# Four chained transformer-like layers on one core: layer 0's two softmax units interleaved, layer 1's keys moved, loads reordered, spare products on TensorE at both ends, a new order of stages

## What is computed

```python
# layer 0: 16 query heads, one key/value head, windowed softmax, gate, RMS norm, centring over tokens
probs = softmax(where(window, q @ k.T * scale, NEG)); attn = (probs @ v) @ Wo + bo
gate = silu(concat(attn, x) @ Wg + bg); out = attn * gate + x * (1 - gate)
x1 = rms(out) * rms_w; x1 = x1 - mean_over_tokens(x1)
# layer 1: each token looks at the three context rows around its index
w = square(relu(q1 . k1[idx-1 .. idx+1] / 4)); x2 = x1 + (w / sum(w) @ v1) @ Wo1
# layer 2: self attention (16 heads, relative bias), then cross attention to the context
xa = x2 + attention(x2, x2); x4 = xa + attention(xa, ctx)
# layer 3: a Mamba2 block in its quadratic form, then cross attention with 8 heads
x5 = x4 + mamba(x4); out = x5 + cross_attention(x5, ctx)
```

## Time and profile before

| | us |
|---|---|
| median of 3 runs | 1412.81 |
| lowest, highest | 1411.97, 1413.31 |
| the profiled execution, own time | 1414.21 |
| the profiled execution, span in the profile | 1411.0 |
| PE busy | 1261.4 (89%) |
| DVE busy | 959.5 (68%) |
| ACT busy | 783.4 (56%) |
| POOL busy | 339.1 (24%) |

### The profile page before, as it was taken

The page is one execution under the profiler, slowest core; times in us unless marked ns, Lnnn a source line. Parts: engine busy times, 40 slices in busy tenths (PEclk is TensorE's granted clock), DMA queues, the critical chain, the costliest instruction groups (busy, mean ns, idle before and its releaser), DMA issues.

```text
span 1411.0 us, 25836 instructions
## 1 busy us (share of the span) xinstructions
PE 1261.4 (89%) x9426; PEld 996.6 (71%) x9426; DVE 959.5 (68%) x1877; ACT 783.4 (56%) x2690; POOL 339.1 (24%) x766
## 2 busy tenths in 40 slices
PE   3567889999999999999999999999999999988755
PEld 2345667877787887877787778788787778766633
DVE  2355466969687877868696968777786869583522
ACT  1124364857565666757475756566675847464411
POOL 0101313231322232232323132223223232302020
PEclk9779999999999999999999999999999999999755
DMA  6901010100001010101000000101010100000000
GB/s 200 331 1 41 1 42 1 34 16 19 29 0 48 0 48 0 45 4 45 4 25 23 15 33 0 48 0 48 0 45 4 45 4 11 27 5 4 4 4 4
DMA packets 28586, 44.38 MB, mean 31 GB/s; under 512 B 4710, under 2 KB 20614, under 8 KB 28044
## 3 DMA queue, kind: packets, MB, share of 16 engines
q1 hardware_dynamic: 26252, 31.41, 7.0%
q0 software_dynamic: 2304, 12.58, 2.5%
HBM read 37.65 MB, written 6.34 MB: 31 GB/s over the span
## 4 chain that ended last, share of the span: by engine, by line
PE 64%; DVE 21%; ACT 11%; issue 2%; DMA 1%; POOL 1%; SPq 0%; POOLq 0%; DVEq 0%; ACTq 0%
PE psum L487 43%; PE psum L481 7%; ACT A L790 5%; ACT sa_p L790 4%; DVE small_ L1003 4%; PE psum L642 3%; PE psum L535 3%; PE psum L694 2%; PE psum L706 2%; PE psum L661 2%; DVE A L997 2%; DVE sa_p L1011 1%; DVE sa_p L997 1%; PE psum L551 1%; DVE A L1088 1%
## 5 line engine op out<-in xcount | busy, mean ns | idle before, releaser
L1279 POOL TENSOR_SCALAR small_<-small_ 128x1 f32<-128x1 f32 x112 | 37.1, 331 | 865.3 <-ACT A L908 382.5
L790 ACT ACTIVATE A<-A,small_ 128x128 f32<-128x128 f32 x384 | 148.6, 393 | 86.0 <-DVE small_ L1004 86.0
L481 PE MATMUL psum<-cst,A 128*128 128x128 f32 x672 | 108.3, 288 | 64.4 <-DVE A L1011 27.0
L783 ACT ACTIVATE A<-psum 128x1024 f32<-128x1024 f32 (+2 forms) x112 | 77.1, 688 | 156.9 <-PE psum L481 109.1
L481 PEld LDWEIGHTS psum<-cst,A 128*128 128x128 f32 x672 | 80.3, 147 | 101.4 <-DVE A L1011 40.5
L1168 DVE SCALAR_TENSOR_TENSOR A<-psum,half_cw,A 128x127 f32<-128x127 f32 (+2 forms) x288 | 75.2, 343 | 41.1 <-ACT A L894 41.1
L790 ACT ACTIVATE sa_p<-sa_p,small_ 128x128 f32<-128x128 f32 x256 | 99.1, 397 | 4.4 <-DVE small_ L1004 4.4
L790 ACT ACTIVATE ca_p<-ca_p,small_ 128x128 f32<-128x128 f32 x256 | 98.7, 391 | 4.8 <-DVE small_ L1004 4.8
L1010 DVE RECIPROCAL small_<-small_ 128x8 f32<-128x8 f32 x112 | 22.3, 199 | 91.1 <-ACT A L790 81.5
L997 DVE TENSOR_TENSOR A<-psum,cst 128x1024 f32<-128x1024 f32 x32 | 39.2, 1225 | 56.9 <-PE psum L535 56.9
L790 ACT ACTIVATION_READ_ACCUMULATOR A<-A,small_ 128x1 f32 x384 | 73.8, 192 | 0.0
(11 more groups left out here) (217 smaller groups left out, 3213.6 us busy)
## 6 DMA issues: line engine op xcount, KB each, us to landing
inT<-in_tokT SPq DMA_DIRECT2D x16, 256.0 KB, 2.9
kv_rows<-A SPq DMA_DIRECT2D x16, 256.0 KB
ctx_in<-in_ctx SPq DMA_DIRECT2D x16, 128.0 KB, 2.1
A<-bias_rows SPq DMA_DIRECT2D x1, 2048.0 KB, 9.3
Wsakv<-in_wsa_kv SPq DMA_DIRECT2D x1, 2048.0 KB, 12.7
Wcakv<-in_wca_kv SPq DMA_DIRECT2D x1, 2048.0 KB, 14.0
ctx_end<-in_tokT SPq DMA_DIRECT2D x16, 128.0 KB, 2.2
out<-x_out SPq DMA_DIRECT2D x16, 128.0 KB, 1.7
```

The source lines that it names most:

```text
L481: mm = pe.transpose(out[:, c * P:(c + 1) * P], src[:, c * P:(c + 1) * P], ident)
L783: return act.activation(out, in_, ACT.Copy)
L790: ins = act.activation(p[:, h * T:(h + 1) * T], p[:, h * T:(h + 1) * T], ACT.Exp, bias=sm(part, "nm", w * HU + h, w * HU + h + 1), accum_o ...
L1279: then(pool.tensor_scalar(t, src, scale, eps, ALU.mult, ALU.add))
```

## The change

It does the following.

- **Units overlapped.** `probs0` becomes two buffers, `R(2)` and `R(1)`. Unit 1's scores wait only until DVE has read unit 0's (`l0_added`), and unit 0's transposes wait until unit 1's scores have been read, since both use `Pa` and `Pb`. PE's order becomes s0, s1, p0, m0, p1, m1.
- **Keys next to the mix.** `keys_values1` becomes a stage `kv1` right behind `l0_m1`, `gate0` waits for its copy, the gather becomes a stage between `gate0` and `back0` on POOL, and SP stores `kv1` first in `load_next`.
- **Loads in order of use.** Tokens and `W0k`, `W0v`, `W0q` go first, PE's wait for the constants moves behind its first products, layer 1's weights go ahead of the bias table's trip, and the first `load_next` goes ahead of the late weights.
- **Bias parts later.** The eight `bias_part` stages move from beside the softmax to `attn0` and the stages behind it.
- **Spare products.** In opening, filling, draining and closing PE runs additional 128x128 by 128x256 products, whose results nobody reads, ahead of the waits of named stages: 21, 10, 16 and 36 of them.
- **New order.** All four strings of `ORDER` change. Two semaphores for sums of squares become one.

```diff
-PART1 = ["inputs", "kv0", "l0_s0", "l0_p0", "l0_m0", "l0_s1", "l0_p1", "l0_m1", "attn0", "gate0", "back0", "center0",
+PART1 = ["inputs", "kv0", "l0_s0", "l0_s1", "l0_p0", "l0_m0", "l0_p1", "l0_m1", "kv1", "attn0", "gate0", "gather", "back0", "center0",
...
-for _g, _stage in enumerate(("l0_m0", "l0_s1", "l0_m1", "gate0", "back0", "center0", "near_k", "turn_o1")):
+for _g, _stage in enumerate(("attn0", "gate0", "back0", "center0", "turn1", "near_q", "near_k", "turn_o1")):
...
-    "PE": "314312434231314134232121413142443143142142321424141",
-    "Activation": "434342134314141232113441323142123242441",
-    "DVE": "412121431444342134133214314442124124134111241",
-    "Pool": "4244141121132",
+    "PE": "3143412314323143241312412311241344314241412132421414",
+    "Activation": "4343243143144121312314312413214213242414",
+    "DVE": "141221341144432413433423122144421411411431214",
+    "Pool": "4221144141132",
+}
+SPARE = {
+    "opening": {"l0_p0": 9, "l0_m0": 1, "l0_m1": 1, "back0": 1, "near_k": 1, "turn_o1": 8},
+    "filling": {"l0_p0": 4, "l0_m0": 1, "back0": 2, "center0": 1, "near_k": 1, "sa_m": 1},
+    "draining": {"m_hat": 2, "m_xbc": 1, "m_heads": 4, "hat3": 2, "q3": 1, "c3_p": 5, "c3_m": 1},
+    "closing": {"m_xbc": 2, "m_seg": 11, "m_xh": 1, "m_heads": 4, "m_back": 2, "hat3": 2, "q3": 1, "c3_p": 12, "c3_m": 1},
 }
...
-        probs0, PT0 = R(2), R(3)
+        probs0, PT0 = (R(2), R(1)), R(3)
...
             def load_next(b, passed):
+                store_kv(passed)
                 sp.wait_ge(sem["near_at"], passed)
                 load_idx(b)
                 sp.wait_ge(sem["out0T"], passed)
-                sp.wait_ge(sem["kv1"], passed)
                 load_tokens(b)
-                store_kv(passed)
...
             load_tokens(0)
+            weights("w0_first", [(W0k, w0_k), (W0v, w0_v), (W0q, w0_q)])
+            sp.dma_start(cst[:], consts).then_inc(sem["const_in"], 16)
...
-            weights("w0_in", [(W0q, w0_q), (W0k, w0_k), (W0v, w0_v), (W0o, w0_o), (W0g, w0_g)])
+            weights("w0_in", [(W0o, w0_o), (W0g, w0_g)])
+            weights("w1_in", [(W1q, w1_q), (W1kv, w1_kv), (W1o, w1_o)])
...
             weights("wsa_in", zip(W2["sa"], (wsa_q, wsa_kv, wsa_o)))
+            load_next(1, 1)
...
-            pe.wait_ge(sem["const_in"], CONSTS_IN)
...
             def bias_table(t):
+                pe.wait_ge(sem["const_in"], CONSTS_IN)
...
             def project0(t):
-                pe.wait_ge(sem["w0_in"], 5 * 16)
+                pe.wait_ge(sem["w0_first"], 3 * 16)
...
-                        need_unit(t, "l0_osb", 0)
+                        need_unit(t, "l0_added", 0)
...
             def turn_probs0(w):
                 def run(t):
+                    if w == 0:
+                        need_unit(t, "l0_added", 1)
+                    else:
+                        need_unit(t, "l0_osb", 0)
                     need_unit(t, "l0_probs", w)
-                    turn(P_1, probs0, HU).then_inc(sem["l0_PT"], 1)
+                    turn(P_1, probs0[w], HU).then_inc(sem["l0_PT"], 1)
...
             def gate0(t):
-                need(t, "attnT_sb")
+                need(t, "attnT_sb", "kv1_sb")
...
             def keys_values1(t):
                 pe.wait_ge(sem["folded"], 1)
-                need(t, "out0T")
...
+            def spare(where, name):
+                to = {"opening": X2["ca"], "filling": X2["ca"], "draining": Pa, "closing": Pa}
+                for _ in range(SPARE.get(where, {}).get(name, 0)):
+                    pe.matmul(to[where][:, 0:D], ident, cst[:, 0:D], start=True, stop=True)
```

More of the change, by code:

```diff
@@ L138 @@
 NAMES = [
-    "const_in", "w0_in", "w1_in", "wsa_in", "late_in",
+    "const_in", "w0_first", "w0_in", "w1_in", "wsa_in", "late_in",
     "prep_exp", "prep_done", "bias_ps", "bias_sb", "skewed_in",
@@ L330, in __init__, with in_turn, run, phase @@
                 self.unit = [value(2, 1), value(2, 2)]
-        def in_turn(eng, order, stages, restart):
-            def run(t, name):
+        def in_turn(eng, order, stages, restart, ahead=lambda where, name: None):
+            def run(t, name, where="loop"):
+                ahead(where, name)
                 for stage in stages.get(name, ()):
                     stage(t)
-            def phase(turns):
+            def phase(turns, where="loop"):
                 for part, name in merged(order, stages, turns):
-                    run(turns[part], name)
+                    run(turns[part], name, where)
             def at(b, i=None, known=None):
@@ L347, in in_turn @@
             for name in OPENING:
-                run(first, name)
+                run(first, name, "opening")
             restart()
-            phase({2: at(0), 1: at(1)})
+            phase({2: at(0), 1: at(1)}, "filling")
             run(first, "fold4")
@@ L360, in in_turn @@
             restart()
-            phase({4: at(B - 2), 3: at(B - 1)})
-            phase({4: at(B - 1)})
+            phase({4: at(B - 2), 3: at(B - 1)}, "draining")
+            phase({4: at(B - 1)}, "closing")
         def need_by(eng):
@@ L456, in _ @@
             load_ctx_end(0)
-            for b in range(1, 4):
+            for b in range(2, 4):
                 load_next(b, b)
@@ L557, in out0 @@
             def out0(t):
+                pe.wait_ge(sem["w0_in"], 2 * 16)
                 need_unit(t, "l0_osb", 1)
@@ L763, in _ @@
                 **{f"l0_m{w}": [mix0(w)] for w in range(2)}, "attn0": [out0], "gate0": [gate0],
-                "back0": [back0, keys_values1], "center0": [center0], "turn1": [turn1], "near_q": [query1],
+                "kv1": [keys_values1], "back0": [back0], "center0": [center0], "turn1": [turn1], "near_q": [query1],
                 "turn_o1": [turn_o1], "out1": [out1],
@@ L770, in _ @@
             }
-            in_turn(pe, ORDER["PE"], stages, lambda: None)
+            def spare(where, name):
+                to = {"opening": X2["ca"], "filling": X2["ca"], "draining": Pa, "closing": Pa}
+                for _ in range(SPARE.get(where, {}).get(name, 0)):
+                    pe.matmul(to[where][:, 0:D], ident, cst[:, 0:D], start=True, stop=True)
+            in_turn(pe, ORDER["PE"], stages, lambda: None, spare)
         @block.scalar
@@ L926, in _ @@
             stages = {
-                **{f"l0_s{w}": [lambda t, w=w: softmax(t, "l0", w, probs0)] for w in range(2)},
+                **{f"l0_s{w}": [lambda t, w=w: softmax(t, "l0", w, probs0[w])] for w in range(2)},
                 **{f"l0_p{w}": [turned0(w)] for w in range(2)}, **{f"l0_m{w}": [mixed0(w)] for w in range(2)},
-                "gate0": [gate], "back0": [squares0, keys_values1], "center0": [squares1], "turn_o1": [turned_o1],
+                "gate0": [gate], "kv1": [keys_values1], "back0": [squares0], "center0": [squares1], "turn_o1": [turned_o1],
                 **layer2("sa"), **layer2("ca"),
@@ L997, in softmax_max @@
                 ins = dve.tensor_tensor(heads(p), heads(scores), extra, ALU.add)
-                if L in LAYER:
+                if L == "c3":
+                    then(ins)
+                else:
                     ins.then_inc(sem[f"{L}_added"], 1)
                     need_unit(t, f"{L}_added", w)
-                else:
-                    then(ins)
                 then(dve.tensor_reduce(mx, heads(p), AX.X, ALU.max))
@@ L1226, in _ @@
                 "inputs": [inputs], "kv0": [project0],
-                **{f"l0_s{w}": [lambda t, w=w: softmax_max(t, "l0", w, probs0, P_1, spread(C("window"), HU))] for w in range(2)},
-                **{f"l0_p{w}": [lambda t, w=w: softmax_norm(t, "l0", w, probs0)] for w in range(2)},
+                **{f"l0_s{w}": [lambda t, w=w: softmax_max(t, "l0", w, probs0[w], P_1, spread(C("window"), HU))] for w in range(2)},
+                **{f"l0_p{w}": [lambda t, w=w: softmax_norm(t, "l0", w, probs0[w])] for w in range(2)},
                 "attn0": [attn0], "gate0": [gate0], "back0": [y0, ctx_hat], "center0": [x1], "turn1": [x1_scaled],
@@ L1303, in rms0 @@
             def rms0(t):
-                need(t, "out0_ssq")
+                need_unit(t, "ssq1", 0)
+                held()
                 rsqrt(1, sm(1, "r"), sm(1, "ssq"), 1.0 / D, 1e-6, "out0_rstd")
             def rms1(t):
-                need(t, "x1_ssq")
+                need_unit(t, "ssq1", 1)
+                held()
                 rsqrt(1, sm(1, "r1"), sm(1, "ssq1"), 1.0 / D, 1.1920929e-07, "x1_rstd")
@@ L1387, in _ @@
             stages = {
-                "inputs": [ctx_rstd], "attn0": [near_rows], "near_q": [gather], "back0": [rms0], "center0": [rms1],
+                "inputs": [ctx_rstd], "attn0": [near_rows], "gather": [gather], "back0": [rms0], "center0": [rms1],
                 "sa_stats": [deviation("sa"), base_sa], "sa_k": [pass_on], "sa_out": [deviation("ca")], "ca_hat": [base_ca],
```

18 lines of the change are left out of this document (8 added, 10 removed).

## The result

The changed kernel takes 1367.61 us (median of 4 runs, 1366.62 to 1370.44) against 1412.39 for the kernel before in the same series: ratio 0.9686, 95% interval 0.9669 to 0.9703, so 3.1% faster. The forecast was 1370.0.

What follows compares the result with a forecast made beforehand. PE bounds the loop's 13 turns; outside it PE waits for chains of small operations at a lower clock. Gains 17 + 9 + 1 + 4 + 12 = 43 us gave 1370 against the 1412.8 median, range 1350 to 1396.

Steps and rivals of the forecast that it cites:

- Start: Opening: DVE becomes the last to be ready, starting at about 12.2; first scores at about 16 instead of 19.07, 3 us gained.
- Two units: Opening: overlapping the two softmax units shortens 29.5 us to a path of 18.4, 11 us gained.
- Spare products in the opening: Nine products overrun PE's idle 4.5 us by 0.5 to 4 us; faster work afterwards was taken to cancel this.
- Rest of the opening: Behind the units to x2: 2.5 us up to out0T, 2 from keys, store and gather leaving the chain, 1 at the tail.
- The later weights behind load_next: Later weights land perhaps 5 us later, but their first user, fold4, comes near 110, so this costs nothing.
- Filling: Filling: second unit and gather leave the chain of part 1 of batch 1; 9 us gained, bounds 0 and 17.6.
- Next stretch: Stretch behind the filling: fold4 is untouched and starts when the filling ends; 1 us gained, bounds -2 and 4.
- Loop: Thirteen PE-bound turns: waits for o1 and x2 go, 0.3 us per turn, 4 in all; bounds 19 gained, 13 lost.
- the order is a real gain: Rival, chance 0.15: in the loop PE's idle time falls by 1.2 of 1.44 us per turn, 12 us beyond forecast: 1358.
- the order costs a little: Rival, chance 0.1: each loop turn takes 0.7 us more, given as 13 us against the 4 gained: 1387.
- Both ends: Draining and closing: spare products raise the clock, 12 of a possible 21 us gained; bounds 19 gained, 6 lost.
- Slower than before: Rival, chance 0.05: DVE work ahead of m_out makes PE wait 3.6 us per turn before hat3, 47 us: about 1417.

Runs made afterwards that it cites:

- experiment 5: The changed kernel with the first loads in the old order, but the first load_next still ahead of the late weights: 1374.64 us, ratio 0.9750.
- experiment 2: The changed kernel with the opening's two units one behind the other again, the overlap kept in filling and loop: 1378.33 us, ratio 0.9774.
- experiment 1: The changed kernel without any of its spare products: 1383.63 us, ratio 0.9813.
- experiment 10: Experiment 9 with the tail of the PE, Activation and DVE order strings changed, so that the waits for c3_p and x2 change places: 1350.08 us, ratio 0.9569.
- experiment 4: The changed kernel with the first load_next put back behind the late weights in SP's queue: 1389.45 us, ratio 0.9840.
- experiment 9: The changed kernel with fold4, POOL's scaling of layer 3's weights, moved behind the next stretch's sa_stats and sa_k stages: 1358.44 us, ratio 0.9647.
- experiment 11: Experiment 9 with 13 more spare products in draining and closing: 1358.39 us, ratio 0.9631.
- experiment 7: The changed kernel with the gather one stage later on POOL, behind back0: 1413.63 us, ratio 1.0020.

## Why the prediction was right, point by point

- **The sum.** 43 forecast, 46.0 measured in the span. Part of this closeness is luck: the opening gave 5.3 us more than forecast and the next stretch 3.2 more, the loop 3.8 less and the filling 1.3 less. (One reading of the earlier trace rows in the prediction is wrong: outside the loop the clock goes from 0.93 down to 0.58, not from 0.79.)
- **Start (3 us, bounds 0 and 4).** Measured 4.3: first scores at 14.80 against 19.07. In the ten kernels with these first loads DVE began between 10.71 and 12.32 and the scores between 14.29 and 15.91, so the term is 3.2 to 4.8, and my 12.2 and 16 lie at its late edge. The other part of it is PE's wait. In experiment 5 PE starts at 12.44, behind three weights, where it started at 14.25 behind five, and has the scores at 17.13 instead of 19.07: 1.9 us. The new order of the loads makes the remaining 2.3.
- **Two units (11, from a path of 18.4).** The path came out at 16.5, the saving at 29.4 - 16.5 = 12.9. The overlap itself gives 8.9 there, and 5.5 to 7.5 at x2 by the execution (experiment 2). The rest of the 12.9 is the bias product that left and the clock.
- **Spare products in the opening (0).** Nine took 4.76 us, 0.53 each, in the changed kernel's profiled execution, below my lower bound of 0.57, but 4.77 to 6.25 in eight others. Without spares unit 0's transposes start 9.8 us behind the first scores (experiment 1), with them 10.0 to 11.5: they overrun by 0.2 to 1.7 us. In return the transposes take 1.06 us instead of 1.94. From the first scores to x2 the kernel without spares takes 44.0 us, the changed one 44.0, and the four others with the same opening 41.3 to 43.2. In the profiled execution of the changed kernel the two cancel; in the other four the spares gain 0.7 to 2.7 us.
- **Rest of the opening (5.5).** Measured 5.1 (from the end of unit 1 to x2, 32.6 before, 27.5 after). The amount is right and the reason is not: I said that keys, store and gather would lie beside output and gate, and the chain still holds the store, 5.46 us where before it took 2.94. What that cost is small, 0.9 us; 2.5 us more went to the low clock behind the norm. In experiment 10, which has neither, the term is 32.6 - 24.1 = 8.5.
- **The later weights behind load_next (0).** This is the step that failed, though the sum does not show it. I asked only who would receive the weights late, and not who was held by their issue. On it hang 17.8 us (experiment 4). That the change had this move in it, and that I counted its effect under other names, is luck.
- **Filling (9, bounds 0 and 17.6).** Measured 7.7. In seven profiled executions that have its spares and do not edit it, experiments 2, 4, 5, 9, 10 and 11 and the changed kernel, it took 51.07 to 55.88. The stretch less PE's busy time is 9.0 to 9.6 us in every one of them; what differs is the busy time, 42.10 at a granted clock of 0.97 (experiment 9) to 46.37 at 0.88 (experiment 10). So the term lies between 4.5 and 9.3, and some 5 us of that are the clock.
- **Next stretch (1).** Measured 4.2, of which some 2.6 are not the change's work on it. Experiments 1, 2, 4 and 5 do not edit this stretch, which has no spares, and took 74.10, 74.19, 74.20 and 74.15; the changed kernel took 71.58. PE's busy time was 62.7 to 62.8 at a clock of 0.91 in them, and 60.18 at 0.95. The difference begins behind the wait of 5.59 us for fold4: the four products (x8) at 124.85 took 4.81 in the changed kernel, and in that of experiment 2 the same four took 6.20, after an identical wait. Whether that is chance or goes with the moment at which the stretch starts is open. Against those four kernels the gain is 1.5 to 1.6.
- **Loop (4; 0.3 a turn).** Measured 0.2 in all. The two waits that I named, 0.55 for o1 and 0.29 for x2, did go, and two others came in their place: 0.38 ahead of `hat3` and 1.20 ahead of the transposes of `c3_p` (`865.26 1.09 PE L491 MATMUL psum<-cst,A 128*128 128x128 f32 x8 [1.20 <-DVE A L1033]`). I had named `hat3` and left it to the rival; `c3_p` I had not seen. Experiment 10 takes the latter away and gains 0.5 a turn, 6.4 us over thirteen. So the rival "the order is a real gain" (1358) did not hold for this order, and the better one got less than half of the 1.2 a turn that it counted on. The rival "the order costs a little" was summed wrongly: 0.7 us more per turn is 9 us, and with my 4 not gained the time is 1383, not 1387.
- **Both ends (12 of 21).** Measured 11.7, and 13.4 by taking the spares away. The rival "the clock does not follow" is refuted by 0.55 against 0.91. Part of the 21 that I left out is the low clock that stayed: in the profiled execution of experiment 9 the closing had a clock of 1.00, these groups took 2.40 and 1.99 instead of 4.09 and 3.70, and the end was 5.6 us shorter, with the same spares.
- **Slower than before.** Not in the changed kernel, and exactly so one POOL slot away (experiment 7).

The Trainium skill's page "TensorE: Matmul & The Clock Gate" (Part 1) says that activity releases the throttle; that holds here for the two ends, where PE does nothing else than spares in the waits and the closing's clock is 0.91 with them and 0.55 without. It adds that the point at which the clock rises differs from run to run of the same kernel. That the clock differs between runs shows here too: four runs of one kernel, experiment 9, lie 10.8 us apart and had granted clocks of 0.995, 0.982, 0.989 and 0.985, the fastest run having the highest. That the clock alone makes these 10.8 us is not shown.

What stays open: why the issues on SP last up to 9.66 us; what decides the clock of the filling and the next stretch in an execution; and whether the 7.7 us of the filling are the overlap's, which was not undone there alone.

## What to carry to other kernels

When a transfer on the critical path is issued from a queue that also issues bulk loads, read that queue's own timeline: a moved issue can carry a gain that the compute engines' rows ascribe to another part. After every gain, ask which transfer was just hidden behind the removed time, and what PE does while it waits: here 8.9 us removed gave 5.5, and most of the missing 3.4 were products at the low clock behind a wait that had grown from 1.28 to 2.20 us. Before a difference between two kernels is given to an edit, compare the stretches that the edit does not touch; here they moved by 2 to 5 us. In a fixed order, a swap is paid by the stage that loses its slot, so read the waits behind a moved stage on every engine, small ones like 0.38 us above all.

## What the runs showed of the hardware

- An instruction that issues a DMA lasted 0.47 us at the start of the opening and up to 9.66 us among loads of 1024 to 2048 KB, and everything behind it on SP waited.
- The same 256 KB store of keys took 2.94, 5.46, 6.95 and 7.35 us in four openings with other transfers beside it, and the gather 4.81, 5.01, 6.36 or 11.12.
- The granted clock in the records of the first microseconds does not tell the speed. In the changed kernel the four query products of layer 0 (x8) took 2.05 us at 8.09, and the same four 1.14 at 113.01, yet the window says 1.00:

```profile
6.00:14.00 8.00, 4.84 (x18) 3.67 (x18) 2.51 (x13) 0.21 (x1) 0.28 (x2) 1.00 0.86 256
```

- A 128x256 product with a constant stationary operand took 0.45 us in the long rows of the closing (4.91 for eleven, 5.45 for twelve), and 0.53 to 0.69 in the opening, where nine took 4.76 to 6.25.
- Behind a wait of 2.94 us products took 1.98 us where they took 1.16 behind one of 0.38 (experiment 7), so a longer wait of PE cost more than its own length.
